# Four matmuls of zeros a step into the attention accumulator, issued while TensorE waits for the weighted values

## What is computed

```python
q = (xn @ Wq + bq).reshape(n, H, DH)          # n = 2500, H = 8 heads, DH = 32
k = (xn @ Wk + bk).reshape(n, H, DH)
v = (xn @ Wv + bv).reshape(n, H, DH)
ep = ef @ We + be
scores = jnp.einsum('ehd,ehd->eh', q[dst], k[src] + ep[:, None, :]) * scale
scores = scores * ew[:, None]
m = jax.ops.segment_max(scores, dst, num_segments=n)
ex = jnp.exp(scores - m[dst])
s = jax.ops.segment_sum(ex, dst, num_segments=n)
attn = ex / s[dst]
out = jax.ops.segment_sum(attn[:, :, None] * v[src], dst, num_segments=n)
out = out.reshape(n, D) @ Wo + bo             # then norm, gelu feed-forward, norm
```

## Time and profile before

| | |
|---|---|
| time, median of 3 runs | 2749.04 us (2747.25 to 2757.36) |
| span of the profiled execution | 2736.8 us |
| PE busy over the span | 2107.6 us (77%) |
| DVE busy | 2183.1 us (80%) |
| ACT busy | 1524.3 us (56%) |
| POOL busy | 1618.3 us (59%) |
| granted TensorE clock, mean | 0.88 |

### The profile page before, as it was taken

How to read it: one execution, slowest core, us unless ns; L and a number is a source line. 1 busy time by engine, 2 the same in 40 slices (tenths; PEclk the granted TensorE clock), 3 DMA queues, 4 the chain that set the end, 5 groups by cost and what they waited for, 6 DMA issues and landing times. The chain is left out here.

```text
span 2736.8 us, 41806 instructions
## 1 busy us (share of the span) xinstructions
PE 2107.6 (77%) x9647; PEld 1611.0 (59%) x9647; DVE 2183.1 (80%) x3415; ACT 1524.3 (56%) x4291; POOL 1618.3 (59%) x1808
## 2 busy tenths in 40 slices
PE   3999999999999999679815666666566666656666
PEld 2787878777777777533314455455455545545555
DVE  6888888888888888645546878878888788878793
ACT  5787888788877887433223444444444444444443
POOL 5666666666666666342246666666666666666642
PEclk8999999999999999889957788878878878887787
DMA  6232222222222222769856666666666666666651
GB/s 203 72 84 81 83 83 83 83 82 84 83 83 81 84 82 84 167 165 253 234 181 168 168 173 175 173 165 173 177 169 175 169 172 176 167 175 170 173 141 45
DMA packets 157414, 379.08 MB, mean 139 GB/s; under 512 B 47810, under 2 KB 63298, under 8 KB 157186
## 3 DMA queue, kind: packets, MB, share of 16 engines
q0 software_dynamic: 100544, 309.00, 40.6%
q1 hardware_dynamic: 44946, 68.53, 8.7%
q10 hardware_dynamic: 11904, 1.34, 0.4%
HBM read 353.36 MB, written 37.07 MB: 143 GB/s over the span
## 5 line engine op out<-in xcount | busy, mean ns | idle before, releaser
L1358 POOL DMA_INDIRECT kv_e<-kv_rows,edge x752 | 716.9, 953 | 408.4 <-issue 223.4
L487 POOL DMA_INDIRECT feat<-in_x_rows,idx x664 | 677.1, 1020 | 236.2 <-issue 234.8
L523 ACT ACTIVATE vsh<-feat,rec_a 128x256 f32<-128x256 f32 x1980 | 806.8, 495 | 8.9 <-DMA feat<-in_x_rows,idx 4.8
L1541 PE MATMUL ps_sum<-kv_e,ident 128*128 128x264 f32 x1504 | 473.8, 477 | 376.9 <-issue 264.2
L1541 PEld LDWEIGHTS ps_sum<-kv_e,ident 128*128 128x128 f32 x1504 | 352.5, 240 | 481.8 <-issue 283.6
L571 PE MATMUL ps_a<-msg,hot 128*128 128x257 f32 x1312 | 409.4, 393 | 4.0 <-issue 4.0
L573 PE MATMUL ps_a<-msg,hot 128*128 128x256 f32 x1312 | 390.6, 379 | 0.1
L575 PE MATMUL ps_a<-msg,hot 128*128 128x192 f32 x1312 | 320.2, 325 | 0.0
L573 PEld LDWEIGHTS ps_a<-msg,hot 128*128 128x128 f32 x1312 | 248.6, 190 | 38.2 <-issue 1.9
L575 PEld LDWEIGHTS ps_a<-msg,hot 128*128 128x128 f32 x1312 | 248.8, 190 | 34.9
L571 PEld LDWEIGHTS ps_a<-msg,hot 128*128 128x128 f32 x1312 | 222.2, 189 | 66.3 <-issue 66.3
(11 more groups left out here) (419 smaller groups left out, 3182.2 us busy)
## 6 DMA issues: line engine op xcount, KB each, us to landing
ef<-in_ef_t SPq DMA_DIRECT2D x84, 256.0 KB
kv_e<-kv_rows,edge POOLq DMA_INDIRECT x752
rows_e<-rows SPq DMA_DIRECT2D x41, 272.0 KB
feat<-in_x_rows,idx POOLq DMA_INDIRECT x664
rows_e<-in_ef_t SPq DMA_DIRECT2D x1, 7446.0 KB, 26.6
kv_rows<-kv SPq DMA_DIRECT2D x20, 260.0 KB, 2.5
rows_e<-in_ef_t SPq DMA_DIRECT2D x1, 3706.0 KB
x<-x_rows SPq DMA_DIRECT2D x23, 128.0 KB
```

The source lines that it names most:

```text
L487: pool.indirect_dma_start(out=feat[:, u, c, 0, :, :].rearrange("p a b -> p (a b)"), out_offset=None, in_=g.x_rows, in_offset=bass.Indirect ...
L523: ins = act.activation(vsh[:, u % TURN, c, j, :, :], feat[:, u % TURN, c, 0, :, :], ACT.Copy, scale=rec_a[:, u % 2, c, 1 + j:2 + j])
L1358: pool.indirect_dma_start(out=kv[:, u, s, :], out_offset=None, in_=g.kv_rows, in_offset=bass.IndirectOffsetOnAxis(ap=edge[:, u, s, DH + 1: ...
L1541: mm = pe.matmul(out, g.ident[:], kv[:, u, s, D:], start=(s == 0), stop=False, skip_group_check=True)
```

## The change

A tile `blank` of 128 by 128 zeros is added and cleared once. At the head of each step TensorE now waits for three marks of VectorE's progress in that step and issues four matmuls between them: zeros by the constant tile `count512` (the numbers 0 to 511), over all 512 columns of the step's accumulator bank. The first of them starts the accumulation; therefore the first sum of values no longer starts it.

```diff
+        blank = sb("blank", [P, P])
...
+            def nothing(u, first=False):
+
+                pe.matmul(ps_o[:, u % BANKS, :], blank[:], g.count512[:], start=first, stop=False, skip_group_check=True)
+
             def step(k, u):
 
                 pe.wait_ge(v_acc, k + 1)
+                pe.wait_ge(v_own, k * 6 + 2)
+                nothing(u, first=True)
+                pe.wait_ge(v_own, k * 6 + 3)
+                nothing(u)
+                pe.wait_ge(v_arg, k + 1)
+                nothing(u)
+                nothing(u)
                 pe.wait_ge(v_fade, k + 1)
...
-                        mm = pe.matmul(out, g.ident[:], kv[:, u, s, D:], start=(s == 0), stop=False,
+                        mm = pe.matmul(out, g.ident[:], kv[:, u, s, D:], start=False, stop=False,
                                        skip_group_check=True)
...
-            dve.memset(ps_o[:], 0.0).then_inc(v_const, 1)
+            dve.memset(ps_o[:], 0.0)
+            dve.memset(blank[:], 0.0).then_inc(v_const, 1)
```

## The result

The changed kernel took 2769.39 us, median of 4 runs (2764.88 to 2773.91), against 2748.14 for the kernel before: a ratio of 1.0076, 95% interval 1.0053 to 1.0098. It is 21 us slower, where 2748 was forecast. The profiled execution has a span of 2772.2 us, 35.4 more than before.

A forecast was written before the change was run, and what follows sets the result against it. Attention was taken as bound by VectorE's work plus one long signal stall a lap. Profiled 2736.8 + 0.1 clearing - 1 clock gain = 2735.9; with the runs' median 12.2 us above the span, 2748, range 2690 to 2798.

The forecast's parts named there:

- What bounds the kernel, and the stalls as a term of their own: Attention lap: VectorE's 44 us, about one of small gaps, and one long stall of 8 to 10 us.
- the 146 that I counted: VectorE's waits for TensorE signals in attention, before L1805, L1783 and L1824: 146.4 us together, expected to stay.
- The zeros hide beside other work: Attention steps: 3.4 us of zero matmuls a step, 320 us in all, fit TensorE's 450 us idle.
- The added waits and the clearing cost nothing: TensorE's new waits in each attention step cost nothing; the one VectorE memset of `blank` 0 to 0.5 us, taken as 0.1.
- The full clock gives 0 to 1 us: Attention's sums of values shrink from 6.40 to 3.83 us where slow, yet VectorE gains only 0 to 1 us, taken 1.
- the last rival: Attention clock stays near 0.8 because zeros do not count as work; priced as held-up work at the lower clock, 2792.
- The step that failed: Attention lap: its length contains no term for TensorE's amount of work, so VectorE's 146.4 us of waits stay.
- The slower rival: Zeros delay `project` beyond its 2.46 us of room before L1805: 2772, or 2792 with the clock low; chance 0.26.
- The faster rival: Attention's late signals depend on TensorE's own activity, so stalls shrink when it never rests: 46 us, 2703; chance 0.34.
- The forecast of no change: Whole kernel: the zeros stay hidden, time 2748 with its own range of 2736 to 2760; chance 0.40.

The follow-up runs named there:

- GpSimd's two waits: Kernel before, GpSimd waiting twice a lap for TensorE's project and outputs signals: 1.0072 with stalls, 0.9996 without; changed kernel with the same waits, without stalls: 1.0001.
- thin zeros: Changed kernel with its zero matmuls 64 columns wide instead of 512, same number of records, against the kernel before: 1.005 with stalls, 1.0000 without.

## Why the prediction was wrong

*What bounds the kernel, and the stalls as a term of their own*: right as far as read. Where they are missing the kernel before takes 225 us less, more than the 146 that I counted: VectorE's idle times in attention were 206 us in all, 34 of them before L1778.

*The zeros hide beside other work*: right as TensorE work. Where signals come in time they cost 0.01%, with the clock at 1.00 (measured with GpSimd's two waits in both kernels; the changed kernel itself was not run there). The forecast of a clock over 0.93 is just met (0.93), and PE busy grew by 262 us, as the 200 or more that I named.

*The added waits and the clearing cost nothing*: right, 1.0002.

*The full clock gives 0 to 1 us*: right on a chip without stalls, where 0.84 or 1.00 made no difference. That zeros might not raise the clock, the last rival, did not come: 0.81 became 0.93.

*The step that failed* is one that I put in a sentence: "TensorE's amount of work appears in none of these terms", and with it that the 146.4 us would stay. I measured the added matmuls by their time alone, set them against idle time, and took the stalls as fixed by GpSimd running out of issues. The runs show that on such chips the stalls grow with the number of TensorE instructions: on the first chip those three waits went from 146.4 to 204.7 us with 32 records more a lap, and on another, between 24 records fewer and 32 more, the attention stage grew from 1251.8 to 1276.8 us. Their number, 64 instructions with the weight loads beside some 276 in a lap, stands in the diff and in the program; I did not treat it as a cost.

*The slower rival* gave 2772 at the full clock and 2769 came. Its number was near, its mechanism was not: no work held up `project`, which ended 1.4 us before VectorE came in the lap above, and thin zeros, busy for a third of the time, cost as much. *The faster rival*, signals sooner from a TensorE that never rests, fell in sign: more instructions mean later signals.

The range, 2690 to 2798, held the time, but by luck: its upper end stood for held-up work, which did not occur. The forecast of no change is refuted; 21 us lie clear of the interval.

*What stays open.* What holds the signals, and why some chips do it and others not. The common traits are few: it is there in attention while gathers run, not in the last lap, and a pause of GpSimd lets the signals out without making the kernel faster. The number of instructions alone does not make a stall: the messages have more of them (5823 records in 1200 us against 3216 in 1260), yet the first L1755 starts at 1419.7 us in the kernel before and at 1407.4 in the one with two waits on a chip without stalls, only 12 us apart. The Trainium skill (Perfetto Trace Analysis, "Per-instruction lifecycle: what the profiler-reported window actually captures") has the semaphore sent after PSUM's acknowledgement; zeros of 64 columns write an eighth as much and cost the same, so the amount written to PSUM is not it. On a chip without stalls (GpSimd's two waits) every semaphore update of TensorE in attention is recorded within 0.02 us of the modelled end. Some queue that takes each TensorE instruction once and drains slowly while gathers run would fit the table; that is argued, not shown.

The nearest rival is the recording itself. Every instruction leaves a record, so the number of instructions and the number of records are the same thing in all these runs, and all timed runs come with a span and a clock. The traces even show that recording differs between the two kinds of chips: each of the eight profiles without stalls holds 38.9 thousand semaphore updates, each of the twelve with stalls 16.4 to 18.2 thousand. The kernel with thin zeros, profiled on both, has 38918 and 17277, and 16726 and 5281 of them in attention; in the messages, which lose little time, it is 18263 and 8806. So where the stalls are, over half of these records are missing. Whether the same cause holds the signals, or the kernel would stall unrecorded too, no run here shows. It also means that a wait named "issue" or "remote" in those profiles may have lost the record that ended it.

Whether instructions of ScalarE would count as well was tried only where there are no stalls, and is open too.

## What to carry to other kernels

Filling an engine's idle time with work that nobody reads is free only if the number of its instructions costs nothing, and not just their time: before adding, ask which wait ends last and whether the engine to be warmed does work on that path. Here a clock of 1.00 instead of 0.84 changed nothing, because VectorE was the bound. Where a signal comes microseconds after its work, look at the same kernel on a second chip before building on the number, and count instructions as well as microseconds.

## What the runs showed of the hardware

- The same kernel takes 2524 us on some chips and 2747 to 2760 us on others, with the same gathers and the same time for each large operation of VectorE (2.29 us for L1755). Most of the difference is waiting for late signals of TensorE: in the two laps shown `project` was done 9.6 and 10.6 us before its waiters went on.
- On the chips with the late signals over half of the trace's semaphore updates are missing (17277 against 38918 for one and the same kernel).
- On a chip without stalls TensorE took 5577 MATMUL records in 950 us instead of 2887, at no cost in time (1.0005).
- During a stall TensorE pauses between matmul records of one sum for up to 2.5 us, with its inputs ready (31 pauses of over 0.3 us in the kernel before, none without stalls).
- A float32 matmul of 512 columns is two records and takes 0.9 us at the full clock (3.60 us for four, granted clock 1.00).
